# A relational graph layer on one core: smaller windows for the edge sums, and matmuls that read gathered tiles in place

## The reference, cut to what matters

```python
def rgcn_layer(x, src, dst, etype, W, W_root, b, num_rels):
    h = jnp.einsum('ni,rio->rno', x, W)
    msg = h[etype, src]
    seg = dst * num_rels + etype
    sums = jax.ops.segment_sum(msg, seg, num_segments=N * num_rels)
    cnt = jax.ops.segment_sum(jnp.ones(msg.shape[0], x.dtype), seg, num_segments=N * num_rels)
    mean = sums / jnp.maximum(cnt, 1.0)[:, None]
    agg = mean.reshape(N, num_rels, do).sum(axis=1)
    return agg + x @ W_root + b
src, dst = (edge_index[0], edge_index[1])
h = rgcn_layer(x, src, dst, edge_type, W1, root1, b1, NUM_RELS)   # 128 -> 256
h = jax.nn.relu(h)
return rgcn_layer(h, src, dst, edge_type, W2, root2, b2, NUM_RELS)  # 256 -> 128
```

## Time and profile before

| | us |
|---|---|
| median of 3 runs | 3190.21 |
| lowest, highest | 3187.76, 3191.98 |
| span of the profiled execution | 3796.5 |

### The profile page before, as it was taken

How to read it: one execution, slowest core, us unless ns; L and a number is a source line. 1 busy time by engine, 2 the same in 40 slices (tenths; PEclk the granted TensorE clock), 3 DMA queues, 4 the chain that set the end, 5 groups by cost and what they waited for, 6 DMA issues and landing times.

```text
span 3796.5 us, 67094 instructions
## 1 busy us (share of the span) xinstructions
PE 2410.4 (63%) x19484; PEld 1719.9 (45%) x19484; DVE 2446.7 (64%) x6233; ACT 1055.3 (28%) x2542; POOL 1893.8 (50%) x2063
## 2 busy tenths in 40 slices
PE   4766689988265655555655559945555555555556
PEld 1222244544244544444444447734444444444446
DVE  5989858961466656656666666646565666656667
ACT  2444411112222222222222224422222222222224
POOL 1877710000555555555555541165555555555555
PEclk8888889989576666666566669956666666666668
DMA  1343410241111111111111111111111111111111
GB/s 51 87 105 99 101 41 1 95 122 39 45 40 40 42 41 42 41 41 42 41 42 42 41 33 62 80 44 42 41 41 42 42 41 42 41 42 42 42 42 29
DMA packets 175229, 192.61 MB, mean 51 GB/s; under 512 B 110526, under 2 KB 141137, under 8 KB 174870
## 3 DMA queue, kind: packets, MB, share of 16 engines
q0 software_dynamic: 50048, 102.60, 9.5%
q10 hardware_dynamic: 84924, 40.88, 4.4%
q1 hardware_dynamic: 39898, 44.85, 3.5%
HBM read 130.49 MB, written 38.06 MB: 44 GB/s over the span
## 4 chain that ended last, share of the span: by engine, by line
PE 41%; DVE 26%; another core or an unknown queue 13%; issue 11%; ACT 3%; ACTq 2%; DVEq 1%; DMA 1%; SPq 1%; POOL 1%; POOLq 0%
PE banks L635 27%; DVE adj L1578 13%; DVE hi_hot L1267 4%; PE banks L552 3%; PE banks L567 3%; PE banks L679 2%; ACT adj L1013 2%; DVE lo_hot L1275 2%; PE banks L691 2%; DVE deg_in L1435 2%; DVEq L1576 1%; DMA adj_copy<-adj 1%; DVE adj L1562 1%; SPq L391 1%
## 5 line engine op out<-in xcount | busy, mean ns | idle before, releaser
L635 PE MATMUL banks<-adj 128*128 128x129 f16 x13280 | 1462.9, 290 | 1127.1 <-ACT adj L1013 600.5
L782 POOL DMA_INDIRECT adj<-table,adj x1564 | 1491.4, 954 | 1077.2 <-SPq L441 623.1
L635 PEld LDWEIGHTS banks<-adj 128*128 128x128 f16 x13280 | 1194.6, 131 | 1399.6 <-ACT adj L1013 815.5
L1578 DVE TENSOR_TENSOR adj<-adj,banks 128x516 f32 x1660 | 1147.3, 691 | 1015.9 <-remote 537.7
L1013 ACT ACTIVATE adj<-adj 128x256 f16 x1660 | 636.8, 412 | 1908.6 <-PE banks L635 1050.9
L1562 DVE TENSOR_SCALAR adj<-adj 128x512 f16<-128x512 f16 x1660 | 594.6, 358 | 0.0
L762 POOL TENSOR_SCALAR lo_hot<-minus_iota,zT 128x128 f16<-128x128 f16 x392 | 315.8, 823 | 166.4 <-PE banks L524 105.0
L524 PE MATMUL banks<-hi_hot,lo_hot 128*128 128x400 f16 x977 | 268.4, 382 | 140.5 <-DVE hi_hot L1267 65.8
L1267 DVE TENSOR_SCALAR hi_hot<-iota,zT 128x400 f16<-128x400 f16 x977 | 270.3, 338 | 36.7 <-PE banks L524 36.1
L524 PEld LDWEIGHTS banks<-hi_hot,lo_hot 128*128 128x128 f16 x977 | 101.9, 104 | 307.0 <-issue 253.1
L567 PE MATMUL banks<-adj,split 128*128 128x512 f16 (+1 forms) x1078 | 216.5, 359 | 0.0
(11 more groups left out here) (238 smaller groups left out, 1266.9 us busy)
## 6 DMA issues: line engine op xcount, KB each, us to landing
adj<-table,adj POOLq DMA_INDIRECT x1564
adj_copy<-adj ACTq DMA_DIRECT2D x25, 800.0 KB, 3.8
adj<-adj_copy SPq DMA_DIRECT2D x6, 2176.0 KB, 16.5
table<-adj SPq DMA_DIRECT2D x25, 512.0 KB, 2.6
adj<-adj_copy SPq DMA_DIRECT2D x1, 3072.0 KB, 10.9
adj<-adj_copy SPq DMA_DIRECT2D x3, 1024.0 KB, 15.3
table<-split SPq DMA_DIRECT2D x6, 256.0 KB, 2.3
out_dram<-xres SPq DMA_DIRECT2D x6, 256.0 KB
```

The lines of the kernel that those rows point to most:

```text
L635: m = e.matmul(ps[:, g * CH // 2:g * CH // 2 + b - a], hot[:, j % NHOT, g * P:g * P + P], edge[:, j % NSTG, a:b], start=(q == 0), stop=(q ...
L782: e.indirect_dma_start(gath[:, (t + 1) % NG, :], None, table, bass.IndirectOffsetOnAxis(ap=index[:, which, t:t + 1].bitcast(U32), axis=0)) ...
L1578: e.tensor_tensor(a, a, ps[:, :].rearrange("p (g d) -> p g d", g=G)[:, :, 0:D + 1], ALU.add).then_inc(accumulated, 1)
```

## The change

The window shrinks from 64 to 16 destinations: 16 x 8 = 128 sums, one group. There are then T + 196 - 1 = 977 steps in a pass instead of 830, each with 2 matmuls instead of 8, an addition of 128 x 129 instead of 128 x 516, and a one-hot matrix of 128 x 128 instead of 128 x 512. Six single banks rotate instead of three pairs, and eight one-hot slots instead of six. `sums` keeps its 200 slots.

ACT no longer copies tiles. The ones column moves into `gath`, whose slots grow from 512 to 516 bytes, and PE reads the tile where it landed: it loads the tile numbers itself, 8 registers every 8 steps, takes the maximum with 1, waits for `landed` against that register, and addresses the moving operand by a register. ACT's three pieces of work on the weights run ahead of the pass. A slot of `gath` is free when PE has used it (`scattered`) and no longer when ACT has copied it.

In the tail nothing is added up ahead of PE any more: ACT scales 3 of the 8 slots of a block, DVE 4, POOL 1, and PE places all 8. `place` is built on POOL by folding the identity.

```diff
-WR, WR_LOG2 = 64, 6
+WR, WR_LOG2 = 16, 4
-        NG, NSTG, NHOT = 16, 6, 6
-        NPAIR = 3
-        sums = carve([P, NW4, G, D + 1])
-        gath = carve([P, NG, D], F16)
-        edge = carve([P, NSTG, D + 1], F16)
-        hot = carve([P, NHOT, G * P // 2], F16)
+        NG, NHOT = 16, 8
+        NSUM = 6
+        sums = carve([P, NW4, D + 1])
+        gath = carve([P, NG, D + 1], F16)
+        hot = carve([P, NHOT, P // 2], F16)
...
+        BY_ACT, BY_POOL, BY_DVE = (0, 3, 6), (2,), (1, 4, 5, 7)
...
-                        e.wait_ge(staged_edges[which], least)
+                        if which:
+                            e.reg_alu(least, least, JR, ALU.add)
+                        e.wait_ge(scattered, least)
...
+            tile_regs = [e.alloc_register(f"tile{i}") for i in range(WORDS)]
+            least = e.alloc_register("least_landed")
             def scatter(which):
                 base = which * JR
                 for j in range(JR):
-                    e.wait_ge(staged_edges[which], j + 1)
+                    if j % WORDS == 0:
+                        n = min(WORDS, JR - j)
+                        e.load(tile_regs[0:n], tile_row[:, j:j + n])
+                    e.reg_alu(least, tile_regs[j % WORDS], 1, ALU.max)
                     e.wait_ge(hot_set, base + j + 1)
-                    if j >= NPAIR:
-                        e.wait_ge(accumulated, base + j - NPAIR + 1)
-                    ps = pair[j % NPAIR]
-                    for g in range(G):
-                        for q, (a, b) in enumerate([(D, 2 * D + 1), (0, D)]):
-                            m = e.matmul(ps[:, g * CH // 2:g * CH // 2 + b - a], hot[:, j % NHOT, g * P:g * P + P],
-                                         edge[:, j % NSTG, a:b], start=(q == 0), stop=(q == 1), skip_group_check=True)
+                    e.wait_ge(landed[which], least)
+                    c = e.snap(tile_regs[j % WORDS], min_val=1, max_val=T) % NG
+                    edge = gath[:, bass.ds(c, 1), :].rearrange("p o f -> p (o f)")
+                    if j >= NSUM:
+                        e.wait_ge(accumulated, base + j - NSUM + 1)
+                    for q, (a, b) in enumerate([(D, 2 * D + 1), (0, D)]):
+                        m = e.matmul(bank[j % NSUM][:, 0:b - a], hot[:, j % NHOT, :], edge[:, a:b],
+                                     start=(q == 0), stop=(q == 1), skip_group_check=True)
                     m.then_inc(scattered, 1)
...
-                for w in range(nb * WPB, (nb + 1) * WPB):
-                    _, _, slots, act_at, dve_at = slots_of(w)
-                    e.wait_ge(scaled_act, act_at)
-                    e.wait_ge(slots_added, dve_at)
-                    for g in slots:
-                        m = e.matmul(to, place[:, w % WPB * G, :], sums[:, w, g, 0:D], start=False,
-                                     stop=(w % WPB == WPB - 1 and g == 3), skip_group_check=True)
+                e.wait_ge(scaled_act, (nb + 1) * len(BY_ACT))
+                e.wait_ge(scaled_dve, (nb + 1) * len(BY_DVE))
+                e.wait_ge(scaled_pool, (nb + 1) * len(BY_POOL))
+                for k in range(WPB):
+                    m = e.matmul(to, place[:, k, :], sums[:, nb * WPB + k, 0:D], start=False, stop=(k == WPB - 1),
+                                 skip_group_check=True)
...
-                    e.activation(edge[:, j % NSTG, 0:2 * D], gath[:, bass.ds(c, 1), :].rearrange("p o f -> p (o f)"),
-                                 ACT.Copy).then_inc(staged_edges[which], 1)
...
-            def add_slots(w):
-                for g in slots_of(w)[1]:
...
+            def scale_slots(nb):
+                for k in BY_DVE:
+                    w = nb * WPB + k
+                    e.tensor_scalar(sums[:, w, 0:D], sums[:, w, 0:D], inv[:, w:w + 1], None, ALU.mult).then_inc(scaled_dve, 1)
```

More of the change, by code:

```diff
@@ L85, in gnn_stack @@
         bank = [banks[:, i, :] for i in range(8)]
-        pair = [banks[:, 2 * i:2 * i + 2, :].rearrange("p a b -> p (a b)") for i in range(4)]
+        turned = [banks[:, 2 * i:2 * i + 2, :].rearrange("p a b -> p (a b)") for i in (2, 3)]
         ident = sb("ident", [P, P], F32)
@@ L275, in gnn_stack @@
         hot_set, scattered, accumulated = (sem(n) for n in ("hot_set", "scattered", "accumulated"))
-        landed, slot_free, staged_edges = (
-            [sem(f"{n}{i}") for i in range(2)] for n in ("landed", "slot_free", "staged_edges"))
+        landed, slot_free = ([sem(f"{n}{i}") for i in range(2)] for n in ("landed", "slot_free"))
         tiles_turned, index_set, last_out, pieces_set, ident8_set = (
@@ L657, in turn_rows @@
             def turn_rows(nb):
[L658 removed]
+                g0 = nb * WPB
                 for h in range(2):
@@ L806, in _ @@
             e.wait_ge(inv_set, 2)
-            for w in range(NW4):
-                e.tensor_scalar(sums[:, w, 2, 0:D], sums[:, w, 2, 0:D], inv[:, w * G + 2:w * G + 3], None,
-                                ALU.mult).then_inc(scaled_pool, 1)
+            for nb in range(NB):
+                for k in BY_POOL:
+                    w = nb * WPB + k
+                    e.tensor_scalar(sums[:, w, 0:D], sums[:, w, 0:D], inv[:, w:w + 1], None, ALU.mult).then_inc(scaled_pool, 1)
         @block.scalar
@@ L998, in _ @@
                 split_high(xres, quad, FX)
-            tile_regs = [e.alloc_register(f"tile{i}") for i in range(REGS)]
-            def stage_edges(which):
-                base = which * JR
-                for j in range(JR):
-                    if j % REGS == 0:
-                        n = min(REGS, JR - j)
-                        e.load(tile_regs[0:n], tile_row[:, j:j + n])
-                    e.reg_alu(least, tile_regs[j % REGS], 1, ALU.max)
-                    e.wait_ge(landed[which], least)
-                    if base + j >= NSTG:
-                        e.wait_ge(scattered, base + j - NSTG + 1)
-                    c = e.snap(tile_regs[j % REGS], min_val=1, max_val=T) % NG
-                    e.activation(edge[:, j % NSTG, 0:2 * D], gath[:, bass.ds(c, 1), :].rearrange("p o f -> p (o f)"),
-                                 ACT.Copy).then_inc(staged_edges[which], 1)
-                    if which == 0 and j >= REGS:
-                        between(j - REGS)
-            def between(t):
-                if t == 34:
-                    e.wait_ge(bound_set, 6)
-                    e.activation(bound[:, 12:16], bound[:, 8:12], ACT.Sqrt).then_inc(bound_root, 1)
-                elif t == 38:
-                    e.wait_ge(scale_set, 1)
-                    e.activation(w1p[:, 0, :, :].rearrange("p r o -> p (r o)"), w1[:, :], ACT.Identity,
-                                 scale=scales[:, 0, 0:1]).then_inc(w_high, 1)
-                elif t == 54:
-                    e.wait_ge(w_low, RR)
-                    e.activation(w2p[:, 0, :, :, :], w2_r[:, :, :, :], ACT.Identity, scale=scales[:, 0, 2:3]).then_inc(w_high, 1)
             e.wait_ge(l3_in, 16 * (3 + HB))
@@ L1084, in _ @@
                 table_rows(nb)
-            stage_edges(1)
             e.wait_ge(inv_set, 2)
-            for w in range(NW4):
-                for g in slots_of(w)[0]:
-                    e.activation(sums[:, w, g, 0:D], sums[:, w, g, 0:D], ACT.Identity,
-                                 scale=inv[:, w * G + g:w * G + g + 1]).then_inc(scaled_act, 1)
+            for nb in range(NB):
+                for k in BY_ACT:
+                    w = nb * WPB + k
+                    e.activation(sums[:, w, 0:D], sums[:, w, 0:D], ACT.Identity, scale=inv[:, w:w + 1]).then_inc(scaled_act, 1)
             def final_rows(b0, b1):
@@ L1755, in final_stats @@
                 own.up()
-            for w in range(2 * WPB):
-                add_slots(w)
+            for nb in range(2):
+                scale_slots(nb)
             for nb in range(NB):
-                for w in range((nb + 2) * WPB, min((nb + 3) * WPB, NW4)):
-                    add_slots(w)
+                if nb + 2 < NB:
+                    scale_slots(nb + 2)
                 final_stats(nb)
```

97 lines of the change are left out of this document (47 added, 50 removed).

## The result

The changed kernel takes 3205.2 us (median of 4 runs, 3203.5 to 3206.0), the kernel before 3190.3 (4 runs, 3187.8 to 3192.0). The ratio is 1.0048, with a 95% interval of 1.0034 to 1.0062: slower by half a per cent. The forecast was 3205.0, from a sum of +15.5 for the tail, +2.2 for planning and -2.9 for the ends of the passes.

What follows compares the result with a forecast made beforehand. POOL's gathers were taken to bound the passes, 1.249 us each, 980.9 us a pass. 3190.2 - 2.9 (pass ends) + 2.2 (planning) + 15.5 (tail) = 3205.0 us; 8-in-10 range 3150 to 3240.

Steps and rivals of the forecast that it cites:

- planning: Stage before the passes: its chunk grows from 318 to 465 steps, +2.2 us, bounds 1.3 and 5.
- the ends of the passes: Last tile's way from gather to finished sum loses ACT and some PE and DVE time: -1.5 us, twice, -2.9.
- The tail's term: Tail blocks go from 6 to 9 float32 matmuls on PE, 1.34 to 2.01 us each: +15.5 us, bounds +13 and +20.
- row blocks: Stage with the same 200 slots and instructions, only other strides; PE's work unchanged: 0 us.
- B: Rival, slower: PE's register loads bound the passes if above 2.8 us each; 3337 us at 3.35 a load; chance 0.12.
- C: Rival, no change: place matmuls overlap DVE better or pass ends gain 5 us each, 3193 us; chance 0.08.
- Pace of the gathers: In the passes POOL's gathers set the pace, 1.249 us each, 980.9 us a pass; PE, DVE and ACT have slack.
- The holes: In the profiled passes, 612 us of gaps explain the profile being 606 us longer; taken for a cost of profiling.
- The last sentence of the forecast: Signs against it: slot waits above some 50 us a pass, gather spacing not 1.249, or a falling median.
- rival A: Faster: the passes are not at the gathers' pace today; 3162 us, in the extreme about 2875; chance 0.20.
- The load: PE's load of 8 registers every 8 steps in a pass: 1.5 us, bounds 0.76 and 3.35.
- ACT: In the passes it loses 830 copies each that ended no wait at this pace: cost 0.

Runs made afterwards that it cites:

- the kernel before again: The kernel before, unaltered, run once more for its profile: 3187.8 us, profile span 3185.9.
- the changed kernel again: The changed kernel, unaltered, run on a chip where the kernel before takes 3189.8 us: 3204.2 us, ratio 1.0035.
- the last one above: The changed kernel with WORDS = 1, one register per load on PE instead of eight, also in planning: 3182.5 us against 3188.6 for the kernel before.

## Why the prediction was right, and where it was not

*The time and its sum.* 3205.0 forecast, 3205.2 measured. Against the kernel before again (on another chip, both without stalls) the changed kernel again has planning +7.0, row blocks +3.1, tail +14.9 and passes -5.6 and -2.7, together +16.8; the forecast had +2.2, 0, +15.5 and twice -1.5. The tail's term, which carries the sum, was right by its mechanism. That the whole fits to 0.2 us is luck, as row blocks were missed and passes gave back more. Against the earlier trace rows planning is +1.4; over all versions but the last one above it lies between 980.3 and 989.5, so that term can't be told from its scatter. Two sums of the rivals are off by little: B's 3337 leaves out the -2.9 and is 3334, and C's passes with ends 5 us shorter give 3198, not 3193.

*Pace of the gathers.* Right, and the step on which all hangs. 1.249 us a gather and 980.9 a pass came out of rows of a disturbed profile. The undisturbed ones have 1.249, 984 to 987 and 981 to 982, and half the gathers shorten both kernels. The Trainium skill ("Perfetto Trace Analysis", Identifying the Most-Contended Engine) would send one to the engine of the highest occupancy, DVE with 786 of 984 us in pass 2; DVE's work was then cut to 480, and the pass became 2.4 us shorter. The trace doesn't bear the rule out here: POOL with 742 us stood behind DVE, because the 0.30 us after each gather are not counted as busy. Nor did the one-hots of a quarter of the columns make gathers shorter: 946 ns in the mean, against 948. The Trainium skill ("SBUF — State Buffer", the box on DVE blocking DMA) says that GpSimd can't write descriptors while DVE runs an operation in a two-port mode; no such wait shows here, and no run tells whether the one-hots are operations of that kind.

*The holes.* Wrong. I took the 606 us of the profile for a cost of profiling. They are stalls that come on one chip in all 13 runs and on two others in none: 3795.4 and 3189 us for the same kernel, and the profile of before again spans 3185.9. The derived 984.0 was right because the runs that were timed had none of the stalls, and by nothing that the reasoning on profiling gave it. The last sentence of the forecast named the other reading (holes that were there without the profiler, and then the median falls), and that is what the chip with stalls shows: 3795.4 to 3709.7, with one wait for four gathers. I gave rival A, under which the kernel gets faster, 0.20 and a mechanism with the wrong size: on such a chip the change gains 86 us, as each pass gets some 50 shorter.

*PE.* The matmuls of a step fit (0.60 apart where nothing holds them, 0.65 forecast). The load was mis-sized: 0.59 us and not 1.5, so 8 steps are 5.4 us and not 6.7. With half the gathers the whole chain needs 0.70 a step, 5.6 for eight, against 7.99: a cover of 30% and not 16%. *DVE:* a sum is 0.289 and not 0.34, a one-hot 0.285 and not 0.25; hidden, as forecast. *ACT:* that its copies ended no wait is wrong as it stands, right in what it costs. In pass 2 of before again PE waits 318.8 us for them, in 475 waits:

```profile
PE banks L635 <- ACT adj L1013: 318.8, 475, 8.1
```

The gathers hide these waits where there are no stalls; where there are, the copies cost 70 to 80 us a pass.

*Ends of the passes.* From the start of the last gather to the last sum it is now 4.5 us instead of 5.3 to 6.6: -0.8 and -2.0, with -1.5 forecast. *Row blocks.* I had 0; they take 188.8 to 190.0 us in the versions with windows of 16, against 186.0 and 187.4 in before. DVE and ACT are busy as long as before, PE 2.3 to 3.8 us longer. The reading in place with 64 has 189.3 to 189.9 as well, so it isn't the strides of 16; which of the shared edits it is was not tried.

*Tail.* Right to 0.8 us, in size and in mechanism: 2.01 us a block as worked out, and five placing matmuls take 15.4 us off it again.

## What to carry to other kernels

Work that is taken from engines which wait for an indirect gather brings nothing while the gathers keep their pace, here one in 1.21 to 1.25 us whether they fetch 64 rows or 128, and a step added on a path at full load (three matmuls of 0.224 us in 25 blocks) costs nearly its full price (15.4 us of 16.8): count gathers first, then edit. Where a profile and the median differ by 19%, time the same kernel on more than one chip before giving the difference to the profiler: this change is 0.4 to 0.5% slower where there are no stalls and, with one wait for four gathers, 2.3% faster on the chip that had them. And compare stretch by stretch, and look where else an edited constant is used: one register a load, meant for the passes, took 20 us off planning.

## What the runs showed of the hardware

- Two levels of time for one program, 3189 us on two chips and 3795 on a third, each used at one time. On the slow one short instructions of PE's and SP's sequencers take 0.70 us in step with each other (a register maximum 33 ns otherwise), in episodes some 85 to 91 PE instructions apart, only in the stretches with gathers. The cause is open; packets of the instruction queue q8 don't go with the episodes.
- A gather of 64 rows takes POOL 0.915 us, one of 128 rows 0.948, and 0.30 us follow each, with or without a wait instruction: 1.21 and 1.25 us apart. So, between 64 and 128 rows, a gather costs by the instruction.
- A register load on PE takes 0.298 us for one register and 0.590 for eight in the passes, but 0.307 and 3.46 in planning (medians).
- PE's granted clock in a pass is 0.50 in the changed kernel, which has PE busy for 41% of it, and 0.74 in before, with 66%; both passes go at the gathers' pace.
